# Linear attention with two normalisations on one core: another order of the last three pairs and of the front

## The reference

```python
xn = group_norm(_gn(x), gn1_w, gn1_b, 32)          # _gn normalises 32 groups of 2 channels too
qkv = einsum('oc,bchw->bohw', qkv_w, xn) + qkv_b   # 3 x 128 rows; 8 heads of 16
q_norm = softmax(q * scale, over the 256 pixels)
k_norm = softmax(k, over the 16 rows of a head)
context = einsum('bhdn,bhen->bhde', k_norm, v)
out = einsum('bhde,bhdn->bhen', context, q_norm)   # 128 rows
out = einsum('oc,bchw->bohw', out_w, out) + out_b  # 64 rows
return x + group_norm(out, gn2_w, gn2_b, 1) + _gn(x)
```

## Time and profile before

| | |
|---|---|
| median of 3 runs | 54.73 us (54.72 to 55.77) |
| the profiled execution | 54.7 us |
| its span in the profile | 52.9 us |
| mean granted TensorE clock | 0.97 |
| TensorE busy | 44.8 us (85%), 517 matmuls |
| VectorE busy | 40.7 us (77%), 132 instructions |
| ScalarE busy | 33.3 us (63%), 111 instructions |
| GpSimd busy | 28.6 us (54%), 66 instructions |
| chain that ended last | PE 62%, DVE 22%, issue 9%, ACT 1% |

### The profile page before, as it was taken

The page is one execution under the profiler, slowest core; times in us unless marked ns, Lnnn a source line. Parts: engine busy times, 40 slices in busy tenths (PEclk is TensorE's granted clock), DMA queues, the critical chain, the costliest instruction groups (busy, mean ns, idle before and its releaser), DMA issues.

```text
span 52.9 us, 1603 instructions
## 1 busy us (share of the span) xinstructions
PE 44.8 (85%) x517; PEld 32.6 (62%) x517; DVE 40.7 (77%) x132; ACT 33.3 (63%) x111; POOL 28.6 (54%) x66
## 2 busy tenths in 40 slices
PE   2999969599896599999999999999999997995200
PEld 2769467466495448858866876884884854843100
DVE  2067999979987996989999989989949937635730
ACT  0173899799095198587868948945946536358400
POOL 5000850085989968999847855864869500041700
PEclk9999999999999999999999999999999999999855
DMA  0598940000000000000200200210020000020222
GB/s 0 165 172 283 366 161 0 0 0 0 0 0 6 0 0 12 0 6 12 95 4 0 99 6 0 67 45 0 0 99 0 0 12 6 0 91 11 96 99 99
DMA packets 2688, 2.66 MB, mean 50 GB/s; under 512 B 244, under 2 KB 2680, under 8 KB 2680
## 3 DMA queue, kind: packets, MB, share of 16 engines
q1 hardware_dynamic: 2528, 2.49, 14.6%
q10 hardware_dynamic: 152, 0.07, 0.6%
HBM read 1.52 MB, written 1.05 MB: 48 GB/s over the span
## 4 chain that ended last, share of the span: by engine, by line
PE 62%; DVE 22%; issue 9%; ACT 1%; POOL 0%; DVEq 0%; ACTq 0%; POOLq 0%
PE o_ps L568 8%; PE q_ps L473 6%; PE k_ps L507 6%; PE v_ps L507 6%; PE o_ps L605 6%; PE o_ps L582 4%; PE v_ps L497 4%; PE q_ps L546 4%; DVE vs L798 4%; PE k_ps L497 4%; PE q_ps L543 3%; PE o_ps L620 3%; DVE kmx L755 3%; DVE res L859 2%; PE o_ps L593 2%
## 5 line engine op out<-in xcount | busy, mean ns | idle before, releaser
L292 POOL TENSOR_TENSOR orstd<-ve,minus_half 128x1 f32<-128x1 f32 x8 | 4.4, 554 | 8.2 <-DVE ve L841 8.2
L273 POOL TENSOR_TENSOR tree<-ek 128x256 f32<-128x256 f32 x7 | 5.1, 722 | 6.0 <-ACT ek L392 6.0
L402 ACT ACTIVATE eq<-q_ps,nqmax 128x256 f32<-128x256 f32 x16 | 7.4, 472 | 0.5 <-DVE nqmax L773 0.5
L415 ACT ACTIVATE fold<-o_ps,rq 128x65 f32<-128x65 f32 x14 | 3.6, 310 | 5.8 <-PE o_ps L582 5.8
L755 DVE TENSOR_REDUCE kmx<-k_ps 128x32 f32<-128x512 f32 x8 | 5.5, 686 | 1.5 <-PE k_ps L507 1.3
L798 DVE TENSOR_TENSOR vs<-v_ps,rks 128x512 f32<-128x512 f32 x8 | 5.5, 691 | 0.7 <-issue 0.4
L392 ACT ACTIVATE ek<-ek 128x512 f32<-128x512 f32 x8 | 5.0, 627 | 1.4 <-DVE ek L764 1.4
L473 PE MATMUL q_ps<-ones 128*128 128x512 f32 x12 | 5.0, 573 | 1.0 <-POOL ones L220 1.0
L764 DVE TENSOR_TENSOR ek<-k_ps,kmx 128x512 f32<-128x512 f32 x8 | 5.5, 683 | 0.1
L773 DVE TENSOR_REDUCE nqmax<-q_ps 128x2 f32<-128x512 f32 x8 | 5.5, 684 | 0.0
L507 PE MATMUL k_ps<-w_all,xn 64*128 64x128 f32 x64 | 5.0, 274 | 0.6 <-DVE xn L729 0.6
(11 more groups left out here) (99 smaller groups left out, 106.9 us busy)
## 6 DMA issues: line engine op xcount, KB each, us to landing
out_dram<-res SPq DMA_DIRECT2D x8, 128.0 KB, 1.7
x_sb<-x_dram SPq DMA_DIRECT2D x1, 512.0 KB, 5.0
x_sb<-x_dram SPq DMA_DIRECT2D x2, 128.0 KB, 2.4
x_sb<-x_dram SPq DMA_DIRECT2D x1, 256.0 KB, 4.0
w_all<-weights_dram SPq DMA_DIRECT2D x1, 224.0 KB, 3.8
mats<-matrices_dram SPq DMA_DIRECT2D x1, 160.0 KB, 4.9
par_avg<-params_dram ACTq DMA_DIRECT2D x1, 67.0 KB, 2.5
brow<-b_qkv_dram ACTq DMA_DIRECT2D x1, 6.0 KB
```

The source lines that it names most:

```text
L273: nc.gpsimd.tensor_tensor(tree[:], e[:, :, 0:8], e[:, :, 8:16], ALU.add).then_inc(tree_step, 1)
L402: last = nc.scalar.activation(eq[:, p % 3, image, :], q_ps[:, image, 0, :], ACT.Exp, bias=nqmax[:, r, image:image + 1], accum_out=qs[:, p ...
```

## The change

It moves calls within the hand-written orders of three engines and takes out two groups of fillers (L656 with two matmuls, L661 with four) and one wait (L655). GpSimd's and SyncE's orders are not touched, and no instruction is added.

At the front, VectorE's `raw_stats(4)` moves from ahead of `key_max(0)` to ahead of `raw_stats(5)`, and `group_variance(2)` from behind `key_shift(1)` to ahead of `key_max(1)`. On TensorE `keys(2)` is issued ahead of `values(1)`.

In the tail, on TensorE `means(5)` and `outputs(5)` come directly behind `queries(7)`, then `values(7)` and `context(6)`. On ScalarE `fold_copy(5)` comes ahead of `key_exp(7)`, and `squares(5)` and `centred(5)` ahead of `query_exp(7)`. On VectorE `key_shift(7)` is ahead of `variance_eps(4)`, `minus_mean(5)` directly behind `last_key_sums`, `query_max(7)` behind `key_norm(7)`, and `output_scale(4)` ahead of `mask_context(6)`.

```diff
-WARM = (7, 5, 3, 6, 2, 4)
+WARM = (7, 5, 3, 6)
@@ ScalarE
+            fold_copy(PAIRS - 3)
             key_exp(PAIRS - 1)
-            fold_copy(PAIRS - 3)
-            query_exp(PAIRS - 1)
             squares(PAIRS - 3)
             centred(PAIRS - 3)
+            query_exp(PAIRS - 1)
@@ TensorE, front
             context(0)
             group_average(3)
+            keys(2)
             values(1)
-            keys(2)
@@ TensorE, tail
             folds(PAIRS - 3)
             queries(PAIRS - 1)
-            pe.wait_ge(ve_ready, PAIRS - 3)
-            warm_up(WARM[4], o_of(PAIRS - 2))
-            context(PAIRS - 2)
-            values(PAIRS - 1)
             means(PAIRS - 3)
             outputs(PAIRS - 3)
-            warm_up(WARM[5], k_ps[:, 1, :, :, :].rearrange("p u c d -> p (u c) d"))
+            values(PAIRS - 1)
+            context(PAIRS - 2)
             context(PAIRS - 1)
@@ VectorE, front
             affine(1)
-            raw_stats(4)
             key_max(0)
             key_shift(0)
             query_max(0)
+            group_variance(2)
             key_max(1)
             key_shift(1)
-            group_variance(2)
             key_norm(0)
             scale_values(0)
+            raw_stats(4)
             raw_stats(5)
@@ VectorE, tail
             key_max(PAIRS - 1)
             mask_context(PAIRS - 3)
-            variance_eps(PAIRS - 4)
             key_shift(PAIRS - 1)
             key_norm(PAIRS - 2)
             scale_values(PAIRS - 2)
+            query_norm(PAIRS - 2)
+            variance_eps(PAIRS - 4)
+            last_key_sums()
+            minus_mean(PAIRS - 3)
+            key_norm(PAIRS - 1)
             query_max(PAIRS - 1)
-            query_norm(PAIRS - 2)
-            last_key_sums()
-            key_norm(PAIRS - 1)
-            minus_mean(PAIRS - 3)
             scale_values(PAIRS - 1)
+            output_scale(PAIRS - 4)
             mask_context(PAIRS - 2)
             query_norm(PAIRS - 1)
             mask_context(PAIRS - 1)
-            output_scale(PAIRS - 4)
             finish(PAIRS - 4)
```

## The result

The changed kernel takes **52.54 us** (median of 4 runs, 52.44 to 52.66) against 54.72. The ratio is 0.9603, 95% interval 0.9574 to 0.9631. The forecast was 52.5. The profiled execution took 52.49 with a span of 50.7, and a mean granted clock of 0.98. Ratios in this text compare only executions within 1.5% of the fastest of the same kernel, so single longer ones (55.77 of the kernel before) don't enter them.

What follows compares the result with a forecast made beforehand. The loop was taken as one rigid TensorE run, so time could come only from the front and tail, where VectorE and TensorE wait for each other. 0.78 + 1.43 = 2.21 off 54.7 gave 52.5 us; 8-in-10 range 52.1 to 53.7.

Steps and rivals of the forecast that it cites:

- The front, 0.78: Ahead of the loop: kmx(2), key maximum of pair 2, starts at 16.10 instead of 16.88, and the loop 0.78 us earlier.
- kmx(0)'s 0.34: Front, VectorE: with raw_stats(4) no longer ahead, the key maximum of pair 0 starts 0.34 us earlier.
- within 0.1: Front, VectorE: group_variance(2) fills the hole ahead of kmx(1), so kmx(1) and ek(1) stay where they were, within 0.1 us.
- the cost of group_variance(2): Front, VectorE: 0.86 us, from its dev at 12.21 to the rks at 13.07, put into the hole ahead of kmx(1).
- The tail, 1.43: Behind the loop: nb(5) no longer waits for outputs(5), so vs(7) starts at 42.49 instead of 43.92, 1.43 us earlier.
- a cost of 0.60 on the path: Tail, VectorE: nqmax(7), moved behind rks(7), takes 0.60 us ahead of vs(7), paid out of the wait removed.
- The fillers and the clock, 0: Tail, TensorE: fillers go, the hole of about 0.75 us before context(7) costs nothing, and the granted clock stays at 1.00.
- the two clock rivals: C and D: TensorE's clock falls in the tail, late or already at its start; chances 0.06 and 0.05.
- A: Front's gain absorbed: keys(2) or pair 4's coefficients late, loop starts where it did; 53.3 us; chance 0.10.
- B: New wait in the tail: fold_copy(5) or outputs(5) late holds up minus_mean(5) and what follows; 53.2 to 53.9 us; chance 0.11.
- C: Clock falls late, at the hole before context(7): 1.7 us more, 54.2, or 55.3 at twice the time; chance 0.06.
- D: Slower: clock falls already at the tail's start; 55.4 to 57.9 us, taken as 56.5; chance 0.05.

Runs made afterwards that it cites:

- e1: Kernel before with only the front's VectorE and TensorE orders changed, tail and its fillers as before: 53.98 us, ratio 0.9864.
- e8: Changed kernel with values(1) ahead of keys(2) on TensorE again: 53.02 us, ratio 0.969; one of six executions took 55.78.
- e2: Kernel before with only the tail orders of all three engines changed and the six tail fillers out: 53.23 us, ratio 0.9729.
- e4: Kernel before with only TensorE's new tail order, without tail fillers; ScalarE and VectorE as before: 54.19 us, ratio 0.9904.
- e5: Kernel before with only VectorE's new tail order; TensorE with its fillers and ScalarE as before: 54.97 us, ratio 1.0048.
- e10: Changed kernel with query_max(7) moved ahead of last_key_sums on VectorE: 52.49 us, ratio 0.9595.
- e6: Changed kernel with two fillers added in TensorE's hole between context(6) and context(7): 52.58 us, ratio 0.9611.
- e3: Kernel before without the six tail fillers and the wait ahead of them: six executions 54.50 to 54.92 us, six 55.52 to 56.49, median 55.22.
- e7: Changed kernel without the nine front fillers between keys(1) and context(0): median 56.22 us, four executions 54.17 to 54.60, eight 56.15 to 57.01.
- e12: Changed kernel with query_max(7) ahead of last_key_sums and mask_context(0) ahead of group variance 3 on VectorE: 51.97 us, ratio 0.9483.
- e9: Changed kernel with group variance 2 behind key_shift(1) on VectorE again, as before: 52.91 us, ratio 0.9659.

## Why the prediction was right, step by step

**The front, 0.78.** Measured 0.78 in the trace and 0.74 by e1. kmx(0)'s 0.34 was right. The claim that kmx(1) stays "within 0.1" was wrong by 0.27 against 10.88. The step had the cost of group_variance(2) too low, at 0.86: from its dev to kmx(1) it is 1.10 (10.05 to 11.15), because its pow_in took 0.42 and not 0.17. What saved the sum is that the moments and the average were late by only 0.07 to 0.12 against the forecast, and that kmx(2), forecast for 16.10, came at 16.12. That the 0.78 came out to the hundredth is luck in part. That keys(2) had to go first was right: e8 shows it.

**The tail, 1.43.** Measured 1.46 from folds(5) to vs(7), and 1.48 by e2. Right, with e2 and e4 behind it: outputs(5) ahead of context(6) and values(7) frees nb(5), and the loop's spacing could be used to time it. Wrong in its parts: nqmax(7) was put down as "a cost of 0.60 on the path". It lies over a pause of VectorE's sequencer of 0.44 that was in the kernel before too, as the 0.42 of issue ahead of vs(7) in the earlier trace rows. The sum came out by luck: my chain rks(7), nqmax(7), vs(7), without pauses, is 0.99 long, and the measured one, with the pause in it, 0.97. The same omission made e4 miss by 0.5, e5 by a part of its 0.25, and, with last_key_sums later than I had it, e10 by 0.33.

**The fillers and the clock, 0.** Right for this change: in e6 fillers in the hole change nothing. But the ground given, that the clock stayed at 1.00 in a window with 0.18 us of work, was thin. It shows one hole of about a microsecond in one execution, with work before it. Where fillers are taken out and the hole stays open, the mean clock is lower in six of twelve executions (e3) or in all (e7). The Trainium skill ("TensorE: Matmul & The Clock Gate", What's actually happening) has activity as what holds the clock up, and e3 and e7 agree. I gave the two clock rivals 0.11 together; they are no mishap but what happens here to an order that drops fillers and leaves the hole open.

**Rivals.** A: out (e1 and e2 add). B: did not occur, though VectorE's order alone (e5) is that rival, 0.25 slower. C and D: did not occur in the four runs of the changed kernel; the one long execution of e8 shows that something like them can.

## What to carry to other kernels

When a hand-written order has a loop whose spacing is known, order the tail like the loop before filling its holes: the loop's offsets then time every step. A fixed "issue" gap in the chain is a term of the sum: ask whether it moves with the work or with the place in the program, and put something useful over it. Take warm-up matmuls out only together with the wait that they cover, and look at every execution's time and clock, not at the best.

## What the runs showed of the hardware

**GpSimd holds up VectorE.** The pow_in of group_variance(2), two elements a partition, took 0.42 in the changed kernel. Here is e12, where it took 0.66:

```profile
10.52 0.74 POOL L273 TENSOR_TENSOR tree<-ek 128x256 f32<-128x256 f32 x1 [3.23 <-ACT ek L392]
10.62 0.66 DVE L706 TENSOR_SCALAR pow_in<-gvar 128x2 f32<-128x2 f32 x1
```

In both it ends 0.02 to 0.03 after GpSimd's tree addition (11.01 and 11.04 in the changed kernel, 11.26 and 11.28 here). It is the same in all eight traces in which this pow_in stands beside that addition: 0.40 to 0.66 us, and an end 0.02 to 0.03 behind the addition's. In e9, where no GpSimd instruction ran beside it, it took 0.17, and in the kernel before too. Nearby VectorE instructions of PSUM operands, gvar for one, were not held. The Trainium skill ("SBUF — State Buffer", Who interferes with whom) describes a pair of ports shared by the two engines, which one of them at a time holds for a whole instruction, VectorE's tensor_scalar in its two-port mode among the users. The traces agree, with 0.23 to 0.49 us as the price. It was not tried by itself.

**A pause in VectorE's program ahead of vs(7),** 0.44 us in every trace, at every order of the instructions around it. The Trainium skill ("Runtime: NRT & Kernel Launch", Instruction fetch mechanics) says that the sequencers fetch their program in blocks and that crossing a boundary is mostly hidden. A pause that stays behind the same number of instructions would fit such a boundary not hidden. In all fourteen traces an 8 KB DMA packet of the kind "instruction" starts 0.6 to 1.0 us after the pause's end, which fits too, though which engine's program it carries is not shown. No run here shows the cause: it would take a kernel with some VectorE instructions more or less ahead of that place.

**The price of the low clock for a whole execution:** e5's profiled run, 69.77 us at 0.58, beside 54.94 to 54.98 at 0.97 to 0.99.
